# One round of the threshold search moves from VectorE to ScalarE in each group of three tiles

## The reference

```python
Q = Xa @ W1
K = Xa @ W3
logits = Q @ W2 @ K.T / TAU
idx = jnp.argsort(-logits, axis=1)
vals = jnp.take_along_axis(logits, idx, axis=1)
csum = jnp.cumsum(jax.nn.softmax(vals, axis=1), axis=1)
k_i = jnp.sum(csum < P_NUC, axis=1) + 1          # smallest set of largest entries with 0.9 of the mass
...
masked = jnp.where(keep, logits, -jnp.inf)
return jax.nn.softmax(masked, axis=1)
```

## Time and profile before

| | before |
|---|---|
| median of 3 runs (us) | 3786.09 |
| lowest and highest run (us) | 3783.11, 3787.79 |
| span of the profiled execution, first to last instruction (us) | 3781.4 |
| busy share of the span: TensorE, VectorE, ScalarE, GpSimd | 78%, 94%, 83%, 10% |
| DMA: moved, mean rate | 292.05 MB, 77 GB/s |
| the two layer steps in the span (us) | some 61 to 1603 and 1606 to 3132 |

### The profile page before, as it was taken

How to read it: one execution, slowest core, us unless ns; L and a number is a source line. 1 busy time by engine, 2 the same in 40 slices (tenths; PEclk the granted TensorE clock), 3 DMA queues, 4 the chain that set the end, 5 groups by cost and what they waited for, 6 DMA issues and landing times. The chain is left out here.

```text
span 3781.4 us, 42418 instructions
## 1 busy us (share of the span) xinstructions
PE 2942.2 (78%) x14004; PEld 2083.2 (55%) x14004; DVE 3553.9 (94%) x4740; ACT 3150.2 (83%) x4561; POOL 360.3 (10%) x417
## 2 busy tenths in 40 slices
PE   6568787786878787648879797888979734799998
PEld 4456666575756666413535354453535424567787
DVE  7999999999999999699999999999999996777887
ACT  6999999999999999389999999999999952345443
POOL 3000000000000000000000000000000005434444
PEclk9689888898989888869989898998989867899999
DMA  2112122212222220032111111111111005355553
GB/s 92 64 55 87 61 93 65 94 54 85 71 78 81 67 87 17 29 133 63 35 41 49 37 46 35 54 37 51 37 41 49 21 5 193 111 176 187 195 205 108
DMA packets 157483, 292.05 MB, mean 77 GB/s; under 512 B 14480, under 2 KB 87248, under 8 KB 153936
## 3 DMA queue, kind: packets, MB, share of 16 engines
q1 hardware_dynamic: 128032, 216.33, 18.2%
q10 hardware_dynamic: 29232, 73.02, 5.5%
HBM read 236.34 MB, written 52.95 MB: 77 GB/s over the span
## 5 line engine op out<-in xcount | busy, mean ns | idle before, releaser
L693 DVE SCALAR_TENSOR_TENSOR s_dump<-s_rows,s_mid 128x3327 bf16<-128x3327 f32 x608 | 2238.8, 3682 | 2.3 <-issue 0.7
L642 ACT ACTIVATE s_adump<-s_rows,s_mid 128x3327 int8<-128x3327 f32 x324 | 995.6, 3073 | 10.6
L648 ACT ACTIVATE s_adump<-s_rows,s_mid 128x3327 int8<-128x3327 f32 x324 | 992.0, 3062 | 0.0
L905 PE MATMUL bank<-x,s_slab 128*128 128x512 f32 x1352 | 633.6, 612 | 0.0
L882 PE MATMUL bank<-kh,qs 128*128 128x512 f16 (+1 forms) x364 | 146.9, 404 | 361.6 <-DVE s_rows L672 351.1
L905 PEld LDWEIGHTS bank<-x,s_slab 128*128 128x128 f32 x1352 | 266.4, 198 | 280.8 <-issue 268.9
L949 PE MATMUL bank<-hb,s_wT 128*128 128x256 f32 x1352 | 356.9, 409 | 69.8 <-ACT s_wT L520 69.7
L949 PE MATMUL bank<-xab,s_wT 128*128 128x256 f32 x1352 | 348.6, 402 | 70.5 <-ACT s_wT L520 70.4
L938 PE MATMUL bank<-ident,s_rows 128*128 128x128 f32 x1352 | 230.5, 298 | 187.3 <-DVE s_rows L747 186.5
L905 PE MATMUL bank<-hb,s_slab 128*128 128x257 f32 x1352 | 353.3, 402 | 0.0
L949 PEld LDWEIGHTS bank<-hb,s_wT 128*128 128x128 f32 x1352 | 261.6, 204 | 119.9 <-ACT s_wT L520 54.2
(11 more groups left out here) (180 smaller groups left out, 4713.8 us busy)
## 6 DMA issues: line engine op xcount, KB each, us to landing
s_slab<-adjT_dram SPq DMA_DIRECT2D x104, 448.0 KB, 4.0
s_slab<-adjT_dram SPq DMA_DIRECT2D x104, 384.0 KB, 3.7
e_adj<-adjR_dram ACTq DMA_DIRECT2D x23, 1664.0 KB, 7.3
strip<-adjR_dram SPq DMA_DIRECT2D x52, 448.0 KB, 3.5
strip<-adjR_dram SPq DMA_DIRECT2D x52, 384.0 KB, 3.3
e_ring<-sc_d SPq DMA_DIRECT2D x72, 256.0 KB, 5.9
sc_d<-e_stage SPq DMA_DIRECT2D x60, 256.0 KB, 2.4
su_d<-s_su_out ACTq DMA_DIRECT2D x26, 256.0 KB, 2.0
```

Source lines behind the costliest of these rows:

```text
L642: nc.scalar.activation(adump[:], row(g, r), ACT.Sign, bias=st(mid, g, 2), accum_out=cnt[:]).then_inc(S["a_eval"], 1)
L648: nc.scalar.activation(adump[:], row(g, r), ACT.Relu, bias=st(mid, g, 2), accum_out=gap[:]).then_inc(S["a_eval"], 1)
L693: nc.vector.scalar_tensor_tensor(out=dump[:], in0=row(g, r), scalar=st(mid, g, r), in1=row(g, r), op0=ALU.is_gt, op1=ALU.mult, accum_out=s ...
L905: ins = nc.tensor.matmul(acc, slab[:, i % NSLAB, j - PIECES[p], :], s_op[:, j, 0:SN], start=False, stop=(j == NT - 1))
```

## The change

In both steps VectorE hands the last round of role 2 to ScalarE. `TAIL` says how many rounds are handed (1 in each step), `HAND` = 18 how many VectorE does of that tile, and `BOTH` = 20 how many ScalarE does in a group: 19 of its own tile and one of the handed tile. ScalarE's own tile is now role 1, the tile of VectorE that stays whole is role 0, the handed one role 2.

- ScalarE, at the start of group g, does the handed round of group g - 1 (`take_on`, two small operations, then one `search` round), then the exponential of its own next tile, which is now the last of the three to be loaded, then `begin` and 19 rounds. The round itself, now in one function `search`, has the same two passes and the same six small operations. `beats` spreads the 38 beats of other work over 40 half rounds; in the last group the first two half rounds have one beat each and the next ten two.
- VectorE alternates its two tiles for 18 rounds and does the 19th of role 0 alone. It cuts role 0 right after its search, ScalarE's tile in beat 2 of the next group and the handed tile in beat 5. Before, it cut two tiles at the end of its search and one in beat 2.
- The tiles load in the order 0, 2, 1, the homes follow from that, the takes start in beat 10 instead of 8 (37 - 9 per tile, `first_take`), the logits in beat 9, and the exponentials of the first two tiles stand in ScalarE's beats 22 and 31.

```diff
+TAIL = (1, 1)
...
 def load_order(g):
-    return [r for r in ((1, 0) if g == LAST else (2, 0, 1)) if r in roles(g)]
+    return [r for r in (0, 2, 1) if r in roles(g)]
 def home(g, r):
-    return 3 * (g % 2) + (2 - r if g == LAST else (r + g // 2) % 3)
+    def slot(k, r):
+        return slot(k - 1, (0, 2, 1).index(r)) if k else r
+    return 3 * (g % 2) + slot(g // 2, r)
...
+    HAND = BISECT - TAIL[s]
+    BOTH = BISECT + TAIL[s]
+    LAST_TAKE = 2 * BISECT - 1
...
+    def first_take(g):
+        return LAST_TAKE - 9 * len(roles(g + 1))
...
+            def begin(g):
+                act.wait_ge(S["exp_done"], LOADS.index((g, 1)) + 1)
+                if g >= 1:
+                    act.wait_ge(S["a_mid"], BOTH * g)
+                nc.scalar.activation(rest[:, 0:1], st(Z, g, 1), ACT.Copy, scale=2.0 * P_NUC).then_inc(S["a_begun"], 1)
+                nc.scalar.activation(less[:, 0:1], st(Z, g, 1), ACT.Copy, scale=-LEAST * 2.0 ** LOG_STEP).then_inc(S["a_begun"], 1)
+                act.wait_ge(S["a_begun"], 4 * g + 2)
+            def take_on(g):
+                act.wait_ge(mid_ready[1], HAND * (g + 1))
+                nc.scalar.activation(rest[:, 1:2], st(Z, g, 2), ACT.Copy, scale=2.0 * P_NUC).then_inc(S["a_begun"], 1)
+                nc.scalar.activation(less[:, 1:2], st(mid, g, 2), ACT.Copy, scale=-1.0).then_inc(S["a_begun"], 1)
+                act.wait_ge(S["a_begun"], 4 * g + 4)
...
             def beats(g, h):
                 if g == LAST:
-                    return (2 * h, 2 * h + 1) if h <= NGRP + 3 else (h + NGRP + 4,)
-                return (h,)
+                    lead = 2 * TAIL[s]
+                    twice = 3 * NGRP + 1 - lead
+                    if h < lead:
+                        return (h,)
+                    b = lead + 2 * (h - lead)
+                    return (b, b + 1) if b <= 3 * NGRP else (h + twice // 2,)
+                return due(h, 0, 2 * (BOTH if g else BISECT), 2 * BISECT)
...
                 if g + 1 < TRIPLES:
-                    when = (20, 29, 37)[-len(roles(g + 1)):]
-                    if b in when:
-                        exponent(3 * (g + 1) + when.index(b))
+                    for p in range(len(roles(g + 1)) - 1):
+                        if b == first_take(g) + 12 + 9 * p:
+                            exponent(3 * (g + 1) + p)
...
+                if g >= 1:
+                    take_on(g - 1)
+                    for it in range(HAND, BISECT):
+                        search(g - 1, 2, it, BOTH * (g - 1) + TAIL[s] + it, next_fill, next_fill)
+                    exponent(3 * g + len(roles(g)) - 1)
+                begin(g)
+                for it in range(FIRST_PART if g == LAST else BISECT):
+                    search(g, 1, it, BOTH * g + it, next_fill, next_fill)
...
             def between(g, b):
                 if g >= 1 and b == 2:
+                    cut(g - 1, 1)
+                if g >= 1 and b == 3:
+                    scale(3 * (g - 1))
+                    scale(3 * (g - 1) + 1)
+                if g >= 1 and b == 2 * TAIL[s] + 3:
                     cut(g - 1, 2)
-                if g >= 1 and b == 3:
-                    for q in roles(g - 1):
-                        scale(3 * (g - 1) + q)
+                if g >= 1 and b == 2 * TAIL[s] + 4:
+                    scale(3 * (g - 1) + 2)
...
+            begin(0, 0)
             for g in range(LAST):
-                begin(g, 0)
                 for it in range(BISECT):
...
+                    evaluate(g, it, 0)
+                    if it == 0:
+                        begin(g, 2)
+                    if 1 <= it <= HAND:
+                        move(g, it - 1, 2)
+                    if it >= HAND:
+                        between(g, 2 * it)
+                        judge(g, it, 0)
+                        between(g, 2 * it + 1)
+                        move(g, it, 0)
+                        continue
+                    judge(g, it, 0)
+                    between(g, 2 * it)
+                    evaluate(g, it, 2)
+                    move(g, it, 0)
+                    judge(g, it, 2)
+                    between(g, 2 * it + 1)
+                begin(g + 1, 0)
                 cut(g, 0)
-                move(g, BISECT - 1, 1)
-                cut(g, 1)
-            begin(LAST, 0)
```

More of the change, by code:

```diff
@@ L390, in layer_step @@
         cnt, gap, base, over, sgn, fac, mean = (sb(tag + n, [P, 1], F32) for n in ("cnt", "gap", "base", "over", "sgn", "fac", "mean"))
+        rest, less = (sb(tag + n, [P, 2], F32) for n in ("rest", "less"))
         u12 = sb(tag + "u12", [P, KC, 2 * D], F32)
@@ new lines, in take_on, with side @@
+            def take_on(g):
[3 more added lines that the diff above has]
+                act.wait_ge(S["a_begun"], 4 * g + 4)
+            def side(it, low, scale, out):
+                last = -1.0 if it + 1 == BISECT else 1.0
+                nc.scalar.activation(out[:], low, ACT.Copy, scale=last * scale).then_inc(S["a_fac"], 1)
@@ new lines, in search @@
+            def search(g, r, it, n, first, second):
+                k = r - 1
+                up, down = rate(it)
+                low = less[:, k:k + 1]
+                nc.scalar.activation(adump[:], row(g, r), ACT.Sign, bias=low, accum_out=cnt[:]).then_inc(S["a_eval"], 1)
+                nc.scalar.activation(base[:], low, ACT.Identity, scale=float(N), bias=rest[:, k:k + 1]).then_inc(S["a_base"], 1)
+                side(it, low, (down - up) / 2, fac)
+                side(it, low, (down + up) / 2, mean)
+                first()
@@ L502, in above @@
                 act.wait_ge(S["a_base"], n + 1)
                 act.wait_ge(S["a_eval"], 2 * n + 1)
[L504 to L506 removed]
+                nc.scalar.activation(over[:], cnt[:], ACT.Identity, scale=low, bias=base[:]).then_inc(S["a_over"], 1)
+                act.wait_ge(S["a_eval"], 2 * n + 1)
+                nc.scalar.activation(adump[:], row(g, r), ACT.Relu, bias=low, accum_out=gap[:]).then_inc(S["a_eval"], 1)
@@ L507, in settle @@
+                second()
                 act.wait_ge(S["a_over"], n + 1)
@@ L637, in _, with next_fill @@
             for g in range(TRIPLES):
[L638 to L644, removed]
-                        fill(g, b)
[L646 to L652, removed]
+                half = 0
+                def next_fill():
+                    nonlocal half
+                    for b in beats(g, half):
+                        fill(g, b)
+                    half += 1
+                if g >= 1:
[6 more added lines that the diff above has]
+                    search(g, 1, it, BOTH * g + it, next_fill, next_fill)
+            for b in range(beats(LAST, half - 1)[-1] + 1, 2 * BISECT):
                 fill(LAST, b)
@@ L846, in _ @@
                 if e == 2:
+                    cut(LAST - 1, 1)
+                    scale(3 * (LAST - 1))
+                    scale(3 * (LAST - 1) + 1)
+                if e == 2 * TAIL[s] + 3:
                     cut(LAST - 1, 2)
-                    for q in roles(LAST - 1):
-                        scale(3 * (LAST - 1) + q)
+                    scale(3 * (LAST - 1) + 2)
                 if s == 0 and e == 8:
@@ L1001, in _ @@
                         loads = len(roles(g + 1))
-                        for n in due(b, 34 - 9 * loads, 34, NCH * loads):
+                        for n in due(b, first_take(g) - 1, LAST_TAKE - 1, NCH * loads):
                             logits(3 * NCH * (g + 1) + n)
```

77 lines of the change are left out of this document (31 added, 46 removed).

## The result

The change makes the kernel slower: 3881.73 us in the median of four runs (3880.45 to 3882.83) against 3785.62 us for the kernel before on the same chip. The ratio is 1.0254, with a 95% interval of 1.0239 to 1.0268. The forecast was 3885 us.

What follows compares the result with a forecast made beforehand. It took ScalarE to become the bound, with little slack beside VectorE. Step 0's +46.6 and step 1's +52.4 us gave +99.0 on a 3781.4 us span, 3880.4; with 4.7 for the median, 3885 us, range 3864 to 3908.

Steps and rivals of the forecast that it cites:

- What bounds the kernel: In groups 1 to 7, ScalarE needs 169.6 us a group in step 0, 168.6 in step 1; slack 2.8 and 2.2.
- Part 1: Each of eight hand-overs a step adds 8.4 us to ScalarE: round 7.71, two activations 0.33, bare waits 0.38.
- The two unhidden waits: At each hand-over, ScalarE's waits for the Relu pass's sum and the moved exponential's sum stand bare, 0.19 us each.
- Part 2: VectorE's group falls from 172.2 to about 168.5 us; it waits some 9 us per group at its beat 2 cut.
- Part 3: ScalarE's waits for TensorE go: 19.3 us in step 0, 15.2 in step 1, half of 3.2 in step 0's last group.
- Part 4: New load order and homes cost nothing; in step 1, ScalarE waits 4.6 us for VectorE's threshold and saves 1.8.
- The end of a step: At the take-over, ScalarE's loss is paid in full, less 2.4 us in step 1; one more beat costs 0.3.
- The sum: Both steps: +46.6 us in step 0 and +52.4 in step 1, together +99.0 on the profiled span of 3781.4.
- (a): In both steps, VectorE stays the bound and the handed round fits ScalarE's gaps: -56 us, 3730; chance 3%.
- (b): In both steps, ScalarE's lead absorbs its lateness: time within 10 us of before; chance 2%.
- (c): In both steps, TensorE still makes ScalarE wait, so the 36 us of waits stay: 3921; chance 10%.

Runs made afterwards that it cites:

- the extra pass: The changed kernel with one more VectorE pass over 128 x 3327, its result unused, in each group of three tiles: 3880.21 us, ratio 1.0246.
- the light round: The changed kernel with separate dumps for ScalarE's two passes and three small threshold-only operations of its round moved to GpSimd: 3797.14 us, ratio 1.0026.

## Why the prediction was right

**What bounds the kernel.** Right, and the number behind it too: 169.6 us a group for ScalarE, taken as length less waits, came out as 169.6 when VectorE's round was left out. The page's 94 and 83% would have said the opposite.

**Part 1, the added round.** The round itself was right: in the changed kernel ScalarE goes from the hand-over's first operation at 227.56 to the exponential behind it at 235.59, 8.03 us, against 7.71 + 0.33 = 8.04 (the sum speaks of four small operations in a round, it has six; the row holds them all). The two unhidden waits are there as well. From the start of the last Relu pass of ScalarE's own tile to the start of its next search it took, at the end of group 1, 403.51 - 396.65 = 6.86 us before:

```profile
396.65 3.08 ACT L648 ACTIVATE s_adump<-s_rows,s_mid 128x3327 int8<-128x3327 f32 x1
...
403.51 0.20 ACT L490 ACTIVATE s_target<-s_Z 128x1 f32<-128x1 f32 x1
```
and takes 417.24 - 402.02 = 15.22 us after:
```profile
402.02 3.08 ACT L530 ACTIVATE s_adump<-s_rows,s_less 128x3327 int8<-128x3327 f32 x1
...
417.24 0.20 ACT L503 ACTIVATE s_rest<-s_Z 128x1 f32<-128x1 f32 x1
```

That is 8.36 us, forecast 8.42, and it is 8.4 at nearly every other hand-over. Yet seven groups grew from 169.6 to 177.5 us, by 7.9 each: the rest of a group came out 0.5 us shorter than length less waits had said. The difference is spread over nearly all of ScalarE's operations, each a few ns shorter (the Relu pass 3060 ns instead of 3063 in the mean); why was not followed. So of the 4.6 us by which step 0 came out below its forecast (42.0 against 46.6), 3.5 lie there and 1.4 in its last group, 92.2 us instead of 94.9, where 1.3 had been allowed; the first hand-over has 0.3 more.

**Part 2, VectorE's saving turns into waiting.** The amount was right: VectorE's 65.7 us of idle time in seven groups are 9.4 each, forecast "some 9" (10.5 in step 1). The place was wrong. I had it wait at its cut in beat 2, and it waits at its takes and at the items instead, 34.3 and 28.9 us. "None of which comes too late for ScalarE" came true, but it asks in one direction only, and TensorE's order works in the other as well; that is what this step left out. VectorE is stopped by TensorE, and TensorE by ScalarE, before VectorE ever reaches the cut. So it is also late at the take-over and waits 11.0 and 11.9 us there, not some 20. None of it changes the sum, as ScalarE is the bound either way, and the extra pass confirmed that.

**Part 3, waits that go.** Right in step 0: of 19.3 us 0.2 are left. In step 1 ScalarE's waits for TensorE fall from 15.2 to 2.9 us, not to nothing. These 2.9 us and the shorter rest of the groups nearly cancel, and so its groups came out at 177.0 us, just as forecast.

**Part 4, order and homes.** Right: the run without a hand-over is at 0.9994. The one wait that was forecast, for VectorE's threshold at the start of group 1 of step 1, is there, at 4.11 us against 4.6:

```profile
1827.66 0.20 ACT L509 ACTIVATE s_rest<-s_Z 128x1 f32<-128x1 f32 x1 [4.11 <-DVE s_mid L743]
```

**The end of a step.** Right: what ScalarE lost was paid in full at the take-over. Step 1 with what leads to it came to 53.2 us, forecast 52.4.

**The sum.** It is closer than its terms. The span grew by 97.3 us, forecast 99.0: step 0 gave 4.6 less, step 1 0.8 more, and the stretch behind them 2.1 more, where nothing was forecast. The median lies 3.0 us above the profiled span and not 4.7, which is the other half of the 3.3 us between 3885 and 3881.7. The range's upper end does not follow from its own terms: 3885 + 6 + 10 is 3901, and 3908 was written. The measured time lies within either.

**The rivals.** (a), VectorE stays the bound, falls with the round left out (30 us gained, not 56) and with the extra pass. (b), the lead hides it, falls with the result itself, 42.0 us at the first take-over after eight hand-overs. (c), TensorE still makes ScalarE wait, falls with ScalarE's waits. The rule of the Trainium skill ("Perfetto Trace Analysis", Identifying the Most-Contended Engine) would have it that the engine with the highest occupancy comes first; over the span that is VectorE before (94%) and after (90%), and after the change a pass more on it costs nothing.

## What to carry to other kernels

Before moving work from one engine to another, take the receiving engine's time in the stage that the move touches, subtract its waits, and compare that with the stage's pace: here the difference was 2.8 us a group and the round 8. A busy share over the whole span says nothing about it. And where a third engine serves two others in one fixed order, each of the two can hold up the other through it. Time saved on one of them can then turn into waiting a group later, as it did here, so look for where the saved time would be spent before counting it as a gain.

## What the runs showed of the hardware

A GpSimd operation on one column that starts within a VectorE pass over a row tile ends just behind that pass. Timelines of both engines in the light round, in the order of time:

```profile
94.41 3.68 DVE L743 SCALAR_TENSOR_TENSOR s_dump<-s_rows,s_mid 128x3327 int8<-128x3327 f32 x1
96.51 1.71 POOL L701 TENSOR_SCALAR s_base<-s_less,s_rest 128x1 f32<-128x1 f32 x1 [2.21 <-ACT s_less L525]
98.26 3.70 DVE L743 SCALAR_TENSOR_TENSOR s_dump<-s_rows,s_mid 128x3327 int8<-128x3327 f32 x1
98.30 0.21 POOL L702 TENSOR_SCALAR s_fac<-s_less 128x1 f32<-128x1 f32 x1
98.59 3.44 POOL L703 TENSOR_SCALAR s_mean<-s_less 128x1 f32<-128x1 f32 x1
```

The first starts in the middle of a pass and ends at 98.22, when the pass has ended at 98.09. The second gets through in 0.21 us. The third takes 3.44 us and ends at 102.03, with the next pass. Three operations that take some 0.7 us when nothing holds them took from 96.51 to 102.03. In this round ScalarE comes to their results only later, at 103.3; where they come later still, it waits, as above.

The whole trace of the light round bears this out. Of its 1020 such operations 465 start within a pass and are held, and each of them ends 0.05 to 0.14 us after that pass. Another 68 start at most 0.04 us after a pass has begun and get through in 0.21 to 0.23 us, while 12 that start as early are among the held ones. Nearly all that start between two passes are short as well. VectorE's pass did not suffer (mean 3.68 us in both), nor did it change with an int8 dump in place of bf16. The Trainium skill ("SBUF — State Buffer", SBUF: two separate sides) says that the port pair which VectorE and GpSimd share is an exclusive lock, held for a whole instruction, and names a VectorE operation with two SBUF inputs among those that take it, against a GpSimd operation that reads SBUF; the pass here has two, and these operations read it. The first and the third operation agree with it; the second, which starts 0.04 us after a pass and is not held up, does not fit unless its start is off by as much, which no run here can settle; the 68 are of its kind.
